# The gate and the experts of a GNN + mixture-of-experts kernel put into one block on one Trainium2 core

## The reference

```python
x = x + _L0_gnn_ref(_layernorm(x), edge_index, ...)      # 6250 nodes of 256 features
xf = _layernorm(x)
H = gelu(xf @ W1 + b1)                                   # 256 -> 1024
probs = softmax(H @ Wg + bg)                             # 8 experts
assign = argmax(probs)
for e in range(8):
    out += where(assign == e, probs[:, e] * (H @ Wd[e] + bd[e]), 0)
x = x + out
```

## Time and profile before

| what | us |
|---|---|
| median of 3 runs | 1804.43 (1803.94 to 1808.53) |
| the profiled execution, its own time | 1802.79 |
| its span, first to last instruction | 1801.0 |
| the gate and what leads to it | about 1212 to 1464 |
| the experts' block | 1468.6 to 1801.0 |
| PE busy in the span | 1567.5 (87%) |
| mean granted TensorE clock | 0.974 |

### The profile page before, as it was taken

How to read it: one execution, slowest core, us unless ns; L and a number is a source line. 1 busy time by engine, 2 the same in 40 slices (tenths; PEclk the granted TensorE clock), 3 DMA queues, 4 the chain that set the end, 5 groups by cost and what they waited for, 6 DMA issues and landing times. The chain is left out here.

```text
span 1801.0 us, 34324 instructions
## 1 busy us (share of the span) xinstructions
PE 1567.5 (87%) x10616; PEld 1124.0 (62%) x10617; DVE 1107.8 (62%) x4023; ACT 923.5 (51%) x1815; POOL 1009.9 (56%) x1066
## 2 busy tenths in 40 slices
PE   0129999999999898989999999977899939999996
PEld 0115666666666697956555555546455528999995
DVE  6588888888878376832334344327577746666663
ACT  0555555555555355733344222217777727777763
POOL 5736677777777202457777777742356632443342
PEclk9999999999999998999999999999999959999998
DMA  8646566655666200488899899928501131111110
GB/s 245 178 141 219 197 212 211 203 196 201 212 213 211 92 0 21 153 287 304 302 307 315 308 337 328 323 80 277 210 29 38 45 107 37 46 46 50 47 49 13
DMA packets 152581, 305.77 MB, mean 170 GB/s; under 512 B 26115, under 2 KB 108005, under 8 KB 144654
## 3 DMA queue, kind: packets, MB, share of 16 engines
q1 hardware_dynamic: 104370, 191.99, 30.6%
q0 software_dynamic: 41744, 105.90, 18.6%
q10 hardware_dynamic: 6348, 6.40, 1.1%
HBM read 212.02 MB, written 99.68 MB: 173 GB/s over the span
## 5 line engine op out<-in xcount | busy, mean ns | idle before, releaser
L1162 POOL DMA_INDIRECT grows<-table_dram,gsrc x680 | 657.3, 967 | 246.5 <-issue 214.9
L1096 PE MATMUL ps<-table,adj 128*128 128x512 f16 x2842 | 707.5, 381 | 4.2 <-PEq L1307 4.2
L1096 PEld LDWEIGHTS ps<-table,adj 128*128 128x128 f16 x2842 | 389.7, 142 | 168.2 <-issue 11.2
L853 ACT ACTIVATE adj<-ps 128x490 f16<-128x490 f32 (+1 forms) x390 | 223.5, 573 | 178.9 <-PE ps L838 174.4
L825 DVE TENSOR_SCALAR oh_k<-iota_k,keyrem 128x246 f16<-128x246 f16 x780 | 237.3, 309 | 0.0
L824 DVE TENSOR_SCALAR oh_r<-iota_r,keyrem 128x128 f16<-128x128 f16 x780 | 213.3, 275 | 26.5 <-PE ps L838 21.6
L1045 PE MATMUL ps<-grows,oh_g 128*128 128x512 f16 x680 | 166.9, 380 | 17.4 <-DMA grows<-table_dram,gsrc 17.2
L1870 ACT ACTIVATE hf<-ps,b1f,unscale 128x256 f32<-128x256 f32 x224 | 123.1, 566 | 86.8 <-PE ps L1841 80.4
L838 PE MATMUL ps<-oh_k,oh_r 128*128 128x245 f16 x780 | 148.4, 273 | 17.5 <-DVE oh_k L825 13.7
L2369 PE MATMUL ps<-wd,h_hi 128*128 x896 | 148.4, 273 | 0.9 <-DVE y L2427 0.9
L1902 DVE SCALAR_TENSOR_TENSOR h_lo<-hf,beta,h_hi 128x256 f16<-128x256 f32 x224 | 104.1, 485 | 58.2 <-ACT h_hi L1865 55.2
(11 more groups left out here) (362 smaller groups left out, 2605.3 us busy)
## 6 DMA issues: line engine op xcount, KB each, us to landing
adj_dram<-adj SPq DMA_DIRECT2D x30, 1568.0 KB
adj<-adj_dram SPq DMA_DIRECT2D x30, 1568.0 KB, 8.4
cv_raw<-fwd SPq DMA_DIRECT2D x64, 256.0 KB, 5.2
table_dram<-table SPq DMA_DIRECT2D x13, 896.0 KB, 4.1
grows<-table_dram,gsrc POOLq DMA_INDIRECT x680
wd_dram<-cv_parts SPq DMA_DIRECT2D x32, 256.0 KB, 5.2
wd<-wd_dram SPq DMA_DIRECT2D x4, 2048.0 KB, 16.2
in_rows<-sorted_rows SPq DMA_DIRECT2D x56, 129.5 KB
```

Source lines behind the costliest of these rows:

```text
L853: act.activation(m.adj[:, q % 3, d0:d0 + wide, :].rearrange("r d c -> r (d c)"), m.ps[:, n % 3, 0:wide * NT], ACT.Copy).then_inc(a.s_adj, 1)
L1096: last = pe.matmul(acc, adj[:, :, c], table[:, c, :], start=c == 0, stop=c == NT - 1)
L1162: pool.indirect_dma_start(m.grows[:, n % GR, j, :], None, m.table_dram, bass.IndirectOffsetOnAxis(ap=m.gsrc[:, g, part * BT + j:part * BT ...
```

## The change

The experts no longer have a block of their own. `experts` builds its tiles and semaphores and returns five functions, one per engine, and the gate's block calls each at the end of that engine's stream. In place of the barrier stand waits: SP waits for all scatters (s_scat), for the filling rows (as before) and for the tile table (a new semaphore, s_tab) ahead of its first load; PE waits for s_probS. POOL, ACT and DVE get no new wait. The body of the five functions is the text of the former block, moved. The second part moves `place` of quad 10 from behind `choose` of quad 11 to the end of the last step.

```diff
 def ffn(nc, m, a, lead):
     m.wd = m.at("wd", m.wd_at, [P, NEXP, KH // 2, 2, 2, C], F16)
     gate(nc, m, a, lead)
-    experts(nc, m, a)
...
+    x_sync, x_gpsimd, x_tensor, x_scalar, x_vector = experts(nc, m, a)
+    s_tab = S("i_tab")
+
     with nc.Block() as block:
...
             sp.wait_ge(s_padded, 16 * (NEXP + 1))
+            sp.wait_ge(s_scat, 16 * NT)
+            sp.wait_ge(s_tab, 1)
+            x_sync(sp)
...
             pool.wait_ge(s_scat, 16 * NT)
+            x_gpsimd(pool)
...
             pe.transpose(m.ps[:NT, 3, 0:P], m.probs[:, :], m.id32[:, :]).then_inc(s_probT, 1)
+            pe.wait_ge(s_probS, 1)
+            x_tensor(pe)
...
             act.activation(lg[:, :, :], lg[:, :, :], ACT.Exp).then_inc(s_ex, 1)
+            x_scalar(act)
...
                     if h == 1 and (n is None or n >= 2):
                         choose(dve, i - 2, par, QT)
+                if n == NQ - 1:
+                    place(dve, i - 2, par, QT)
...
             for i in range(NQ - 2, NQ):
                 choose(dve, i, i % 2, tiles(i), LB if i < NQ - 1 else LASTB)
-                place(dve, i - 1, (i - 1) % 2, tiles(i - 1))
+                if i == NQ - 1:
+                    place(dve, i - 1, (i - 1) % 2, tiles(i - 1))
             place(dve, NQ - 1, (NQ - 1) % 2, tiles(NQ - 1))
...
-            link(dve.tensor_copy(m.tile_exp[0:1, :], te[:, :]))
+            dve.tensor_copy(m.tile_exp[0:1, :], te[:, :]).then_inc(s_tab, 1)
...
             dve.tensor_copy(probT[:, :], m.ps[:NT, 3, 0:P]).then_inc(s_probS, 1)
+            x_vector(dve)
...
 def experts(nc, m, a):
...
-    with nc.Block() as block:
-        @block.sync
-        def _(sp):
-            def load(i, q):
+
+    def sync(sp):
+        def load(i, q):
...
+    return sync, gpsimd, tensor, scalar, vector
```

More of the change, by code:

```diff
@@ L2311, in experts @@
     DB = 5
-    with nc.Block() as block:
-        @block.sync
-        def _(sp):
-            def load(i, q):
-                for j in range(2):
[L2318 to L2359, removed]
-                for j in range(2):
[L2361 to L2436, removed]
-            with dve.Fori(0, (NPAIR - 2) // 2) as k:
-                dve_hidden(dve, m, u, 2 * k + 1, 1, 2, 2)
-                results(2 * k, 0, k)
-                dve_hidden(dve, m, u, 2 * k + 2, 0, 2, 2)
-                results(2 * k + 1, 1, k)
-            dve_hidden(dve, m, u, NPAIR - 1, 1, 2, 0)
-            results(NPAIR - 2, 0, NPAIR // 2 - 1)
-            results(NPAIR - 1, 1, NPAIR // 2 - 1)
@@ new lines, in sync @@
+    def sync(sp):
+        def load(i, q):
+            for j in range(2):
+                at = sp.value_load(m.tile_row[0:1, bass.ds(2 * i + j, 1)], min_val=0, max_val=NEXP * REG)
+                sp.dma_start(r[:, q, j, :], m.sorted_rows[bass.ds(at, P), :]).then_inc(s_row[q], 16)
+        for i in range(RB4):
+            load(i, i)
+            if i == 0:
+                sp.dma_start(bd[:, :, :].rearrange("p e c -> p (e c)"), bass.AP(a.fbd.tensor, 0, [[0, P], [1, NEXP * C]])).then_inc(s_bd, 16)
+        with sp.Fori(1, NPAIR // RB4) as k:
+            for q in range(RB4):
+                sp.wait_ge(s_used, k * RB4 + (q + 1 - RB4))
+                load(k * RB4 + q, q)
@@ new lines, in gpsimd @@
+    def gpsimd(pool):
+        pool.wait_ge(m.s_prob, 16)
+        for i in range(NPAIR + 1):
+            par, q = i % 2, i % RB4
+            if i >= 2:
+                pool.wait_ge(s_st[par], 32 * (i // 2))
+                pool.sem_inc(s_used, 1)
+            if i < NPAIR:
+                pool.wait_ge(s_row[q], 32 * (i // RB4 + 1))
+                for j in range(2):
+                    token = bass.IndirectOffsetOnAxis(ap=r[:, q, j, C:C + 1].bitcast(I32), axis=0)
+                    pool.indirect_dma_start(pr[:, par, j, :], None, m.prob_dram, token).then_inc(s_gx[par], 16)
+            if i >= 1:
+                pool.wait_ge(s_out, i + 2)
+                for j in range(2):
+                    pool.indirect_dma_start(a.out, bass.IndirectOffsetOnAxis(ap=r[:, (i - 1) % RB4, j, C:C + 1].bitcast(I32), axis=0),
+                                            outt[:, 1 - par, j, :], None, bounds_check=N - 1, oob_is_err=False).then_inc(s_st[1 - par], 16)
+        for par in range(2):
+            pool.wait_ge(s_st[par], 32 * (NPAIR // 2))
@@ new lines, in tensor, with transpose, down, step @@
+    def tensor(pe):
+        pe_ahead(pe, u)
+        def transpose(i, par, q, uses):
+            pe.wait_ge(s_row[q], uses)
+            pe_transpose(pe, m, u, i, lambda j, k: r[:, q, j, k * P:(k + 1) * P], 2)
+        def down(pe, i, par):
+            for j in range(2):
+                e = pe.value_load(m.tile_exp[0:1, bass.ds(2 * i + j, 1)], min_val=0, max_val=NEXP - 1)
+                if j == 0:
+                    pe.wait_ge(u.split, KH * i + KH * (u.first + 2))
+                pe.wait_ge(s_y, 2 * i + (j + 1))
+                for k in range(KH):
+                    w_hi = m.wd[:, bass.ds(e, 1), k // 2, 0, k % 2, :].rearrange("p a c -> p (a c)")
+                    w_lo = m.wd[:, bass.ds(e, 1), k // 2, 1, k % 2, :].rearrange("p a c -> p (a c)")
+                    for q, (h, w) in enumerate(((m.h_hi, w_hi), (m.h_hi, w_lo), (m.h_lo, w_hi))):
+                        last = pe.matmul(m.ps[:, DB + j, 0:C], h[:, par, k, j * P:(j + 1) * P], w,
+                                         start=q == 0 and k == 0, stop=q == 2 and k == KH - 1)
+            last.then_inc(u.done, 1)
+        def step(i, q, k):
+            par = q % 2
+            pe_hidden(pe, m, u, i, par, 2, {1: lambda: transpose(i + 1, 1 - par, (q + 1) % RB4, k * 32 + 32 * (1 + (q + 1) // RB4))})
+            down(pe, i - 1, 1 - par)
+        transpose(0, 0, 0, 32)
+        pe_hidden(pe, m, u, 0, 0, 2, {1: lambda: transpose(1, 1, 1, 32)})
+        pe.wait_ge(m.s_wd, 16 * NEXP // 2)
+        with pe.Fori(0, (NPAIR - 2) // RB4) as k:
+            for q in range(1, RB4 + 1):
+                step(k * RB4 + q, q, k)
+        last = (NPAIR - 2) // RB4
+        for q in range(1, NPAIR - 1 - last * RB4):
+            step(last * RB4 + q, q, last)
+        pe_hidden(pe, m, u, NPAIR - 1, 1, 2, {})
+        down(pe, NPAIR - 2, 0)
+        down(pe, NPAIR - 1, 1)
@@ new lines, in scalar, with residual @@
+    def scalar(act):
+        def residual(i, par, q, k):
+            act.wait_ge(s_row[q], 32 * k + 32)
+            act.wait_ge(s_out, i + (1 - 2 + 2))
+            for j in range(2):
+                last = act.activation(x1t[:, par, j, :], r[:, q, j, 0:C], ACT.Identity,
+                                      bias=r[:, q, j, C + 2:C + 3], scale=r[:, q, j, C + 1:C + 2])
+            last.then_inc(s_xt1, 1)
+        act.sem_inc(u.gelu, UB)
+        act_xt(act, m, u, 0, 0, 2)
+        act_hidden(act, m, u, 0, 0, 2, 2)
+        residual(0, 0, 0, 0)
+        with act.Fori(0, (NPAIR - 4) // 4) as k:
+            for q in range(1, 5):
+                act_hidden(act, m, u, 4 * k + q, q % 2, 2, 2)
+                residual(4 * k + q, q % 2, q % 4, k + q // 4)
+        for i in range((NPAIR - 4) // 4 * 4 + 1, NPAIR):
+            act_hidden(act, m, u, i, i % 2, 2, 2 if i < NPAIR - 1 else 0)
+            residual(i, i % 2, i % 4, i // 4)
@@ new lines, in vector, with results @@
+    def vector(dve):
+        dve_ahead(dve, u)
+        dve.sem_inc(s_y, 2)
+        dve.sem_inc(s_out, 2)
+        def results(i, par, k):
+            e = [dve.value_load(m.tile_exp[0:1, bass.ds(2 * i + j, 1)], min_val=0, max_val=NEXP - 1) for j in range(2)]
+            dve.wait_ge(u.done, i + (u.first + 3))
+            dve.wait_ge(s_gx[par], k * 32 + 32)
+            dve.wait_ge(s_xt1, i + 1)
+            for j in range(2):
+                dve.scalar_tensor_tensor(y[:, par, j, :], m.ps[:, DB + j, 0:C], m.inv_g[:, 0:1],
+                                         bd[:, bass.ds(e[j], 1), :].rearrange("p a c -> p (a c)"), ALU.mult, ALU.add).then_inc(s_y, 1)
+            for j in range(2):
+                dve.wait_ge(s_y, 2 * i + (j + 3))
+                last = dve.scalar_tensor_tensor(outt[:, par, j, :], y[:, par, j, :], pr[:, par, j, :], x1t[:, par, j, :], ALU.mult, ALU.add)
+            last.then_inc(s_out, 1)
+        dve_xt(dve, m, u, 0, 0, 2)
+        dve_hidden(dve, m, u, 0, 0, 2, 2)
+        dve.wait_ge(s_bd, 16)
+        with dve.Fori(0, (NPAIR - 2) // 2) as k:
+            dve_hidden(dve, m, u, 2 * k + 1, 1, 2, 2)
+            results(2 * k, 0, k)
+            dve_hidden(dve, m, u, 2 * k + 2, 0, 2, 2)
+            results(2 * k + 1, 1, k)
+        dve_hidden(dve, m, u, NPAIR - 1, 1, 2, 0)
+        results(NPAIR - 2, 0, NPAIR // 2 - 1)
+        results(NPAIR - 1, 1, NPAIR // 2 - 1)
```

## The result

The changed kernel takes 1800.16 us (median of 6 runs, 1798.67 to 1800.99), the kernel before 1804.69 us beside it. The ratio is 0.9974 with a 95% interval of 0.9964 to 0.9985, so about 4.7 us less (2.7 to 6.5). Forecast were 1792.4 us and 12 us less. The measured time lies just outside the stated range (1789.5 to 1800).

What follows compares the result with a forecast made beforehand. PE's work bounds the two long stretches; the change touches only the gap between them, ended by POOL's DRAIN, and the tail. -4.05 - 1.75 - 6.2 = -12.0 us gave 1790.8 for the profiled execution, median 1792.4, range 1789.5 to 1800.

Steps and rivals of the forecast that it cites:

- Part 1: Between gate and experts: without the barrier SP needn't wait for POOL's DRAIN and reads the tile table 4.05 us sooner.
- Part 2: Gate's tail: moving quad 10's place brings the last scatter and filling rows, so the first table read, 1.75 us sooner.
- The exception that the prediction named: Last tile's scatter: GpSimd's transfers get all 16 DMA engines; then both start gains sum to 4.45 us instead of 5.8.
- Part 3: Kernel's end: the merged block's one DRAIN of POOL would cost 3.0 us instead of 9.19, so 6.2 us less.
- It looks as if the list is emptied on the way each time it is full: POOL's last DRAIN: of 161 indirect DMAs only 34 to 38 would be left to pay for, 3.0 us.
- The term of -6.2 us: Kernel's end: the gain from a shorter last DRAIN of POOL, with a spread from -5.5 to -6.4 us.
- The period of 127 and 123 DMAs: POOL's list size, read from both aggregations' DRAINs: 254 is twice 127, 246 twice 123.
- The drain that only moves: Kernel's end: DRAIN costs 0.082 us per DMA up to 161, giving back 4.07 us; 1802.7 us in all, 13%.
- Half a list at a time: POOL's last DRAIN: a full list drops 64, leaving 98 DMAs, 8.0 us; the end gains 1.2, 1797.4 us, 14%.
- The two ends of the term: POOL's last DRAIN: 3.0 us if the list is emptied when full, 13.2 us if all 161 DMAs are paid for.
- Slower by PE's loop: Experts' loop on PE: six rounds may each wait for instructions, 25 us in all; 1817.6 us, 5%.
- The price of 4.2 us for a late jump: Linear block's end: the wait taken as what each of the PE loop's six rounds might cost.

Runs made afterwards that it cites:

- the block alone: Changed kernel with quad 10 placed behind choose of quad 11 again, so only the blocks are merged; 0.9977 (0.9968 to 0.9986) of the kernel before.
- place_only: Kernel before, still two blocks, with only quad 10's place moved to the end of the last step; 0.9998 (0.9988 to 1.0007) of the kernel before.
- experiments 5 and 6: Changed kernel with two extra gathers at pair 13 (1794.93 us), 1 or 26; changed kernel with the last scatter over 128 partitions (1.002 and 0.9986), also with added DRAINs.
- experiment 5: Changed kernel with two extra 4-byte gathers per row by POOL at pair 13, 1 or 26; at pair 13 1794.93 us, 0.9945 of the kernel before.
- agg_wait: Kernel before, with POOL waiting behind each aggregation's gathers until PE has used the last gathered rows; one run, 2075.99 us beside 2063.8.
- drains: Changed kernel with a POOL DRAIN every four pairs and one ahead of the last pair's store; 1790.33 us, 0.9918 (0.9904 to 0.9931) of the kernel before.

## Why the prediction was wrong

- **Part 1, right.** 4.05 us forecast, 4.18 measured with the block alone. It was POOL's DRAIN, as SP's waits said.
- **Part 2, right for the scatters, too large for the filling rows.** 1.75 us forecast for both. The scatters' landing came 1.8 us sooner and the filling rows 1.4 in place_only, and in the merged block, where the filling rows decide, the moved place gave 1.17. The 1.72 us of place_only hit the number by way of the scatters and the DRAIN. Not seen was SP's last read of padi behind the last scatter: 1.9 to 2.1 us in the four traces with the moved place on the first chip, under 0.5 without it. On the other chips the longest read took 1.3 to 1.8 us, with the place moved or not, and 0.6 where the last tile has 128 rows. That two engines work on the scatter stands: the Trainium skill's rule in "DMA: Bandwidth & Descriptors", section on why a DMA increments its semaphore by 16, by which 106 rows go over two engines, agrees with experiments 5 and 6. The exception that the prediction named is one for some direct copies there, and this indirect scatter did not follow it.
- **Part 3, the step that failed.** It read rightly that a merged block pays its DRAIN once, at the end, and 0.082 us per DMA. The failing step is "It looks as if the list is emptied on the way each time it is full". It isn't emptied. It loses what stands in front of and with the first DMA without a successor on its semaphore. In the merged block that is the last scatter: 49 fall, 161 - 49 = 112 are left, exactly as many as without the gate. The term of -6.2 us was +0.03.
- **How it was misread.** The period of 127 and 123 DMAs came from two rows and isn't one. The first aggregation's 9.1 us behind the last gather were taken for 111 DMAs; with POOL waiting first its DRAIN takes 8.40 us, 102 of them (what the other 0.7 us were isn't shown). And the 65 indirect DMAs that the preparation issues ahead of its 357 gathers were left out. With 68 and 102 left, both aggregations fit three drops of 85, not two of a whole list.
- **Rivals.** The drain that only moves (13%): no, the 49 scatters are never paid for. Half a list at a time (14%): no, 112 are left and not 98, and experiment 5 has 108, 60 and 10. That its 68 and 102 for the aggregations are what agg_wait measured is luck; worked out exactly, its rule gives 67 and 101 (323 and 357 less 4 x 64). The two ends of the term, 3.0 and 13.2, held the truth between them, but the case that came, "the end stays as it is", had no chance of its own; it would have been -5.8 us, 1798.6. Slower by PE's loop: PE was busy 200 of 200 us. The price of 4.2 us for a late jump was read from a wait at a block's end; no run here shows such a jump.
- **The sum.** With 9.2 in place of 3.0 the forecast is -5.8 us, and the trace has -5.8 behind quad 9. That they meet is luck: the join gave 0.45 us less than forecast, and the 0.5 us of the stretch behind it are scatter. The medians' 4.7 (2.7 to 6.5) include that. Why the untouched front of the profiled executions differed by up to 2.6 us between kernels (1438.85 to 1441.49) was not tried.

The version that beats both is `drains`: 1790.33 us, 14 us or 0.8% below before by the ratio's 0.9918; on another chip the ratio was 0.9984 (0.9954 to 1.0014).

## What to carry to other kernels

A DRAIN at a block's end is not the barrier's formality: read its row, for the last block too, and ask what it counts. If it counts POOL's indirect DMAs, pay it in small parts where POOL waits for others. How much a merged block pays at its end depends on what has fallen from the list by then, so compute it from the order of the DMAs and their semaphores. And when a law is read from two or three rows, give the outcome "the term doesn't change" a place among the cases.

## What the runs showed of the hardware

- A DRAIN of POOL took 0.082 to 0.086 us per indirect DMA still on its list: 0.86 us for 10, 4.07 for 49, 5.63 for 68, 8.40 for 102, 9.27 for 113; whether they had landed long ago made no difference.
- The list held 113 DMAs of 128 rows each, but only 108 with one of 106 rows among them. The next made it lose all up to and with the first one without a later one on its semaphore. Two extra gathers changed the last DRAIN from 9.2 to 8.9, 5.0 or 0.9 us by their place alone.
- Where 49 to 104 DMAs fell, the DMA that found the list full was issued 0.4 to 1.8 us late (0.75 us behind the one before where 0.31 was usual, 4.91 where 3.65 was, 0.93, 2.04 and 2.09 where 0.30 was). In the second aggregation no such delay was seen.
- A scatter of 106 rows landed in 6.8 to 7.3 us, where the median of all 49 was 2.6 to 2.7, with the DMA engines at the share of two (0.12 to 0.13) near its end; spread over 128 partitions, the join behind it was 1.5 to 2.0 us shorter.
- A register load by SP, usually 0.27 us, took 1.3 to 2.1 us when it came behind such a scatter, and 0.6 behind one of 128 rows. What it waits for there is open.
